# A Mamba state read out in the scan's own layout: half scans in place in PSUM, products with broadcast rows of C, accumulating transposes

## The reference

```
def step(h, ins):
    dt_t, u_t, B_t, C_t = ins
    h = jnp.exp(dt_t[..., None] * A) * h + (dt_t * u_t)[..., None] * B_t[:, None, :]
    y_t = jnp.einsum('bdn,bn->bd', h, C_t)
    return (h, y_t)
_, ys = jax.lax.scan(step, h0, xs)
y = jnp.moveaxis(ys, 0, 1) + u * Dp
y = y * jax.nn.silu(z)
```

## Time and profile before

| | |
|---|---|
| median of 3 runs | 2786.99 us (2777.39 to 2789.61) |
| the profiled execution's own time | 2776.09 us |
| its span | 2774.3 us |
| VectorE busy | 2444.0 us (88%) |
| TensorE busy | 2240.5 us (81%) |
| GpSimd busy | 1963.9 us (71%) |
| ScalarE busy | 1442.7 us (52%) |
| scan, 512 times | 1167.3 us |
| read_out, 1920 + 128 operations | 783.9 + 52.3 us |
| mean granted TensorE clock | 0.895 of full speed |
| DMA | 17.1% of 16 engines, 57 GB/s |

### The profile page before, as it was taken

How to read it: one execution, slowest core, us unless ns; L and a number is a source line. 1 busy time by engine, 2 the same in 40 slices (tenths; PEclk the granted TensorE clock), 3 DMA queues, 4 the chain that set the end, 5 groups by cost and what they waited for, 6 DMA issues and landing times. The chain is left out here.

```text
span 2774.3 us, 39442 instructions
## 1 busy us (share of the span) xinstructions
PE 2240.5 (81%) x10405; PEld 1427.0 (51%) x10405; DVE 2444.0 (88%) x4116; ACT 1442.7 (52%) x2468; POOL 1963.9 (71%) x1437
## 2 busy tenths in 40 slices
PE   3677888889788887978878797887978888897767
PEld 1344555555555454555545455554555555555544
DVE  1798998999899998999999899999989989999963
ACT  2545546555555555555565454655545555555423
POOL 1667868777776877768787686877777687777743
PEclk6778998989899898989989898998989989898989
DMA  2222121211212111121211112121121111112100
GB/s 77 68 69 65 54 70 50 66 54 54 69 46 69 52 54 63 54 69 46 69 54 54 61 53 69 53 69 46 54 69 53 61 54 58 57 54 71 46 25 4
DMA packets 83131, 158.16 MB, mean 57 GB/s; under 512 B 14420, under 2 KB 49076, under 8 KB 83012
## 3 DMA queue, kind: packets, MB, share of 16 engines
q1 hardware_dynamic: 83012, 157.01, 17.1%
HBM read 151.69 MB, written 5.29 MB: 57 GB/s over the span
## 5 line engine op out<-in xcount | busy, mean ns | idle before, releaser
L421 POOL TENSOR_TENSOR bt<-v,bb 128x1024 f32<-128x1024 f32 x512 | 1207.9, 2361 | 368.9 <-DVE h L773 366.1
L773 DVE TENSOR_TENSOR_SCAN h<-psA,bt 128x1024 f32<-128x1024 f32 x512 | 1167.3, 2280 | 70.6 <-issue 34.2
L598 ACT ACTIVATE psA<-dt,aneg 128x511 f32<-128x511 f32 x1024 | 665.0, 681 | 1037.7 <-DVE h L773 1034.6
L984 PE MATMUL psH<-ident,h 128*128 128x128 f32 x4096 | 657.2, 303 | 238.3 <-DVE acc L794 215.5
L794 DVE SCALAR_TENSOR_TENSOR acc<-psH,cc,acc 128x256 f32<-128x256 f32 x1920 | 783.9, 468 | 7.3 <-PE psH L984 7.1
L984 PEld LDWEIGHTS psH<-ident,h 128*128 128x128 f32 x4096 | 512.3, 154 | 530.2 <-DVE acc L794 354.9
L521 POOL TENSOR_TENSOR act<-pf,gf 128x512 f32<-128x512 f32 x288 | 365.9, 1270 | 149.0 <-DVE pf L878 128.6
L1067 PE MATMUL F<-h2T,w 128*128 128x512 f32 x576 | 347.5, 688 | 101.6 <-DVE pf L878 99.4
L1111 PEld LDWEIGHTS F<-w,act 128*128 128x128 f32 x2304 | 312.2, 201 | 110.2 <-issue 102.7
L1111 PE MATMUL F<-w,act 128*128 128x128 f32 x2304 | 322.4, 286 | 5.9 <-DVE facc L892 5.9
L1070 PE MATMUL F<-h2T,w 128*128 128x512 f32 x576 | 307.1, 616 | 0.0
(11 more groups left out here) (140 smaller groups left out, 1892.0 us busy)
## 6 DMA issues: line engine op xcount, KB each, us to landing
bb<-b_rows SPq DMA_DIRECT2D x256, 512.0 KB, 3.6
x<-in_L_attn_x SPq DMA_DIRECT2D x16, 256.0 KB, 3.3
xR<-in_L_attn_x SPq DMA_DIRECT2D x16, 256.0 KB, 2.9
out_x<-osb SPq DMA_DIRECT2D x16, 256.0 KB, 3.7
w<-in_L_ffn_ew SPq DMA_DIRECT2D x2, 1024.0 KB
modA<-mod_table SPq DMA_DIRECT2D x16, 128.0 KB, 3.6
modF<-mod_table SPq DMA_DIRECT2D x32, 64.0 KB, 2.6
b_rows<-xd SPq DMA_DIRECT2D x32, 32.0 KB, 1.6
```

The lines of the kernel that those rows point to most:

```text
L421: g.tensor_tensor(bt[:, n % 2, :, :], v[d][:, :, :], bb[:, n // 2 % 2, n % 2, :].unsqueeze(1).broadcast_to([P, NH, T]), ALU.mult).then_inc ...
L598: s.activation(decay[:, half, lo:hi], dt_[d][:, half, lo:hi], ACT.Exp, scale=aneg[d][:, half, n:n + 1]).then_inc(a_s, 1)
L773: w.tensor_tensor_scan(h[:, n % 2, :, :].rearrange("p k t -> p (k t)")[:, order], psA[:, order], bt[:, n % 2, :, :].rearrange("p k t -> p ...
L984: last = m.transpose(psH[:, i * E + half * P:i * E + half * P + P], h[:, n % 2, half, i * P:i * P + P], ident[:, :])
```

## The change

The read-out stays in the layout of the scan. In a slot, for each half: a scan of 512 elements *in place* in psA (so psA holds the state and not the decay), then g = psA * (row of C, broadcast over the partitions by a second DMA, `cb`) into SBUF. TensorE turns g by transposes that accumulate over the 16 states in `psY` (which takes the place of psH). After 16 states ScalarE copies psY into acc (`keep_y`), and `yg` now lies in acc's memory. `exps` of a half of step s+1 waits for the product g of that half of step s. C comes with B from one product (40 rows in place of 24), so CP and its copy go, and Z moves one slot earlier. The zero column goes.

```diff
-U_AT, XD_AT, DT_AT, LN1P_AT, CP_AT, Z_AT, V_AT = 0, 6, 7, 9, 9, 10, 11
+U_AT, XD_AT, DT_AT, LN1P_AT, Z_AT, V_AT = 0, 6, 7, 9, 9, 11
...
                 sp.dma_start(bb[:, pair % 2, :, :].rearrange("p n t -> p (n t)"), src.broadcast_to([P, 2 * T]))\
                     .then_inc(bb_in[pair % 2], 16)
+                wait(sp, g_s, 2 * used)
+                src = bc_dram[d, N + 2 * pair:N + 2 * pair + 2, :].rearrange("n t -> (n t)").unsqueeze(0)
+                sp.dma_start(cb[:, pair % 2, :, :].rearrange("p n t -> p (n t)"), src.broadcast_to([P, 2 * T]))\
+                    .then_inc(cb_in[pair % 2], 16)
...
             def bmul(step, d, n):
-                wait(pool, h_s, step - 1)
+                wait(pool, h_s, NH * (step - 1))
...
             def exps(step, b, d, n):
-                wait(act_e, h_s, step)
-                lo, hi, first = (1, T, 0) if d == 0 else (0, T - 1, T - 1)
-                decay = psA[:, :].rearrange("p (k t) -> p k t", t=T)
                 if n == 0:
                     act_e.wait_ge(dt_s, 2 * b + d + 1)
-                    s.activation(decay[:, :, first:first + 1], zero[:, :, :], ACT.Copy).then_inc(a_s, 1)
                 for half in range(NH):
-                    s.activation(decay[:, half, lo:hi], dt_[d][:, half, lo:hi], ACT.Exp,
+                    wait(act_e, g_s, NH * (step - 1) + half + 1)
+                    s.activation(psA[:, half * T:half * T + T], dt_[d][:, half, :], ACT.Exp,
                                  scale=aneg[d][:, half, n:n + 1]).then_inc(a_s, 1)
+
+            def keep_y(b, d):
+                act_e.wait_ge(y_s, STEPS * b + N * (d + 1))
+                wait(act_e, F2_full, (DOWN + NE) * (b - 1) + PROJ + 1)
+                for half in range(NH):
+                    s.activation(yg[d][:, half, :], psY[:, half * T:half * T + T], ACT.Copy).then_inc(acc_s, 1)
...
-                if k == CP_AT:
-                    take(b, piece(d, CP))
-                    s.activation(cc[d][:, :, :], psP[:, 0:NT * N], ACT.Copy).then_inc(pP_free, 1)
...
+                    if slot == 0 and ffn:
+                        keep_y(b - 1, 1)
+                    if slot == N and scan:
+                        keep_y(b, 0)
...
-            def scan(step, d, n, unit):
-                dve.wait_ge(a_s, NH * (step + 1) + unit)
+            def scan(step, d, n):
+                order = slice(None) if d == 0 else slice(None, None, -1)
                 dve.wait_ge(bt_s, step + 1)
-                wait(dve, pH_full, 2 * step - 2)
-                order = slice(None) if d == 0 else slice(None, None, -1)
-                w.tensor_tensor_scan(h[:, n % 2, :, :].rearrange("p k t -> p (k t)")[:, order], psA[:, order],
-                                     bt[:, n % 2, :, :].rearrange("p k t -> p (k t)")[:, order],
-                                     0.0, ALU.mult, ALU.add).then_inc(h_s, 1)
+                for half in range(NH):
+                    dve.wait_ge(a_s, NH * step + half + 1)
+                    ah = psA[:, half * T:half * T + T][:, order]
+                    w.tensor_tensor_scan(ah, ah, bt[:, n % 2, half, :][:, order], 0.0, ALU.mult, ALU.add)\
+                        .then_inc(h_s, 1)
+
+            def read_out(step, b, d, n):
+                wait(dve, y_s, step - 1)
+                if n % 2 == 0:
+                    dve.wait_ge(cb_in[n // 2 % 2], 128 * b + 64 * d + 16 * (n // 4) + 16)
+                for half in range(NH):
+                    dve.wait_ge(h_s, NH * step + half + 1)
+                    w.tensor_tensor(g_[:, n % 2, half, :], psA[:, half * T:half * T + T], cb[:, n // 2 % 2, n % 2, :],
+                                    ALU.mult).then_inc(g_s, 1)
...
-            def tr_h(step, n):
+            def sum_y(step, kept, n):
+                if n == 0:
+                    wait(pe, acc_s, kept)
+                for half in range(NH):
+                    pe.wait_ge(g_s, NH * step + half + 1)
+                    for i in range(NT):
+                        last = m.matmul(psY[:, half * T + i * P:half * T + i * P + P],
+                                        g_[:, n % 2, half, i * P:i * P + P], ident[:, :], is_transpose=True,
+                                        start=(n == 0 and i == 0), stop=(n == N - 1),
+                                        skip_group_check=True)
+                last.then_inc(y_s, 1)
...
```

More of the change, by code:

```diff
@@ L19 @@
 KINDS = 6
-U, XD, DT, CP, Z = 0, 2, 3, 5, 6
-PREP = 8
+U, XD, DT, Z = 0, 2, 3, 5
+PREP = 7
 PIECES = 1 + 2 * PREP + NH
@@ L132, in adaln_mamba_moe @@
         zs = [sb(f"zs{d}", [P, NH, T]) for d in range(2)]
-        xd = sb("xd", [R + N, T])
-        cc = [sb(f"cc{d}", [P, NT, N]) for d in range(2)]
+        xd = sb("xd", [R + 2 * N, T])
         xb = sb("xb", [P, NH, T])
@@ L141, in adaln_mamba_moe @@
         bt = sb("bt", [P, 2, NH, T])
-        zero = sb("zero", [P, NH, 1])
-        h = sb("h", [P, 2, NH, T])
-        acc = [sb(f"acc{d}", [P, NT, E]) for d in range(2)]
+        cb = sb("cb", [P, 2, 2, T])
+        g_ = sb("g", [P, 2, NH, T])
+        acc = [sb(f"acc{d}", [P, NH, NT, P]) for d in range(2)]
         def part(buf, rows, lo, shape):
@@ L234, in adaln_mamba_moe @@
         bb_in = [sem(f"bb_in{k}") for k in range(2)]
+        cb_in = [sem(f"cb_in{k}") for k in range(2)]
         bt_s = sem("bt_s")
@@ L237, in adaln_mamba_moe @@
         h_s = sem("h_s")
-        pH_full = sem("pH_full")
+        g_s = sem("g_s")
+        y_s = sem("y_s")
         acc_s = sem("acc_s")
@@ L264, in adaln_mamba_moe @@
         MOD_STEPS = 12
-        CONSTS = 10
+        CONSTS = 9
         block = ctx.enter_context(nc.Block())
@@ L930, in body @@
                     if scan_:
-                        scan(step, slot // N, slot % N, 2 * b + 1 + slot // N)
-                    if slot > 0 and scan_:
-                        read_out(step - 1, (slot - 1) // N, (slot - 1) % N, b)
-                    elif slot == 0 and ffn:
-                        read_out(step - 1, 1, N - 1, b - 1)
+                        scan(step, slot // N, slot % N)
+                        read_out(step, b, slot // N, slot % N)
                     if scan_:
@@ L976, in _ @@
             pe.wait_ge(halved, 7)
-            def tr_h(step, n):
-                pe.wait_ge(h_s, step + 1)
-                for i in range(NT):
-                    if i % 2 == 0:
-                        wait(pe, acc_s, NT * step - NT + i + 2)
-                    for half in range(NH):
-                        last = m.transpose(psH[:, i * E + half * P:i * E + half * P + P],
-                                           h[:, n % 2, half, i * P:i * P + P], ident[:, :])
-                    if i % 2 == 1:
-                        last.then_inc(pH_full, 1)
+            def sum_y(step, kept, n):
[9 more added lines that the diff above has]
+                last.then_inc(y_s, 1)
             def prep(b, d, k):
@@ L1006, in prep @@
                     for half in range(NH):
-                        last = m.matmul(psP[0:R + N, :], wxT[d][:, half, 0:R + N], u[d][:, half, :],
+                        last = m.matmul(psP[0:R + 2 * N, :], wxT[d][:, half, :], u[d][:, half, :],
                                         start=(half == 0), stop=(half == NH - 1))
-                    last.then_inc(pP_full, 1)
-                if k == CP_AT:
-                    open_piece(CP)
-                    for i in range(NT):
-                        for half in range(NH):
-                            last = m.matmul(psP[:, i * N:(i + 1) * N], u[d][:, half, i * P:i * P + P],
-                                            wxT[d][:, half, R + N:R + 2 * N], start=(half == 0), stop=(half == NH - 1))
                     last.then_inc(pP_full, 1)
@@ L1028, in skip_and_turn @@
                 for i in range(NT):
-                    last = m.matmul(bank[:, i * P:i * P + P], acc[d][:, i, half * P:half * P + P], ident[:, :],
+                    last = m.matmul(bank[:, i * P:i * P + P], acc[d][:, half, i, :], ident[:, :],
                                     start=False, stop=(i == NT - 1))
@@ L1121, in body @@
                     step = STEPS * b + slot
-                    if (slot > 0 and scan_) or (slot == 0 and ffn):
-                        tr_h(step - 1, (slot - 1) % N)
+                    if slot > 0 and scan_:
+                        sum_y(step - 1, 4 * b + 2 * ((slot - 1) // N), (slot - 1) % N)
+                    elif slot == 0 and ffn:
+                        sum_y(step - 1, 4 * b - 2, N - 1)
                     if ffn:
```

59 lines of the change are left out of this document (21 added, 38 removed).

## The result

| | before | changed |
|---|---|---|
| median | 2785.81 us (2777.39 to 2789.61, 4 runs) | 2804.83 us (2802.63 to 2809.09, 4 runs) |
| profiled execution, its span | 2776.09, 2774.3 | 2805.65, 2803.9 |
| VectorE busy | 2444.0 | 2302.2 |
| TensorE busy, mean granted clock | 2240.5, 0.895 | 2152.3, 0.916 |
| DMA | 17.1%, 57 GB/s | 31.0%, 105 GB/s |

The ratio is 1.0077, 95% interval 1.0054 to 1.0100: slower, as forecast, but by 0.8% and not by 2.2%.

The account below looks back on a forecast made before the run. VectorE was taken as the bound, with ScalarE's chain just beneath it in up slots. +4.34 per pass over 15 passes (+65), less 4 in pass 0, gave +61: 2837, forecast 2848; own range 2825 to 2880, stated range 2785 to 2925.

Parts of the forecast that it names:

- slot 31: Last slot of a pass: 3.47, then 3.49 from last facc over the loop's branch to next scan: 6.96.
- rival B: Half scans cost exactly their elements, 1.07 each: -4.2 per pass, 2785, no change; chance 8%.
- The chain: In up slots, from g over exponentials and tf to pf: at least 5.44 us pf to pf, before at least 4.77.
- rivals A: Half scans cost more than half: +58, 2906, or 2935 if the products pay more as well; chance 14%.
- Rival D: VectorE stays the bound in up slots, which shrink to 4.07 plus side work: 2672; chance 8%.
- Rival C: TensorE's new idle time in up slots costs it its clock, facc waits: +50 to +100, about 2920; chance 6%.
- Slot 29: ScalarE's 5.10 with logarithm and two table loads, about 0.35 more for the tanh of Z: 5.45.
- Slots 0 to 6: Start of a pass: 30.67 us where it was 31.54 before, -0.87 per pass.
- Slot 10: 4.07, the gate 2.24 and now a silu of Z, 0.60: 6.91, before 6.60.
- the 0.4% that I added: The median of before lies 0.4% above its profiled execution, so 2837 was raised to a forecast of 2848.
- the second broadcast DMA: 512 KB per two slots, issued at least 7.4 + 2.27 us before use, against 3.6 to landing: hidden.
- keep_y: Two ScalarE copies of 0.6 at slots 0 and 16, ahead of exponentials that wait for g anyway: hidden.

Follow-up runs that it names:

- experiment 9: The kernel before with its loop over the 13 middle batches written out: 2727.01 us, ratio 0.9786.
- experiment 10: The changed kernel with its loop over the 13 middle batches written out: 2785.02 us, ratio 0.9990 against the kernel before.
- Experiment 3: The changed kernel with Z put back one slot later, as in the kernel before: 2809.80 us, ratio 1.0081.
- Experiment 1: The changed kernel with the experts' tanh and copy (tf, gf) ahead of the exponentials on ScalarE in up slots 10 to 27: 2683.25 us, ratio 0.9625.
- experiment 8: The kernel before with one more ScalarE wait: exponentials for step s+1 start only after the first two readings of step s-1; 2984.21 us, ratio 1.0687.
- experiment 122: Not a run number: the 122 us by which Experiment 1, the changed kernel with tf and gf ahead of the exponentials, is below 2805; measured 2683.25 us.
- Experiment 7: The kernel of Experiment 1 with, besides, the first tanh of Z ahead of the logarithm on ScalarE: 2672.69 us, ratio 0.9592.

## Why the prediction was wrong in size

**The step that failed: slot 31.** It read "from the last facc over the loop's branch to the next scan 3.49 as before". Those 3.49 were taken for a constant and were not. The measured -2.90 of this slot splits so. VectorE's own work falls from 5.38 (the shortest slot 31 of experiment 9) to 4.47 (that of experiment 10): -0.91, which is about the forecast's -1.00. TensorE's lateness, 5.02 - 4.35 = 0.67, is gone. The pause was 2.64 and is 1.32: -1.32. The last two, 2.0 per pass, were not in the sum. Experiment 3 ties them to Z's move: with Z back in its place slot 31 is 8.34. The forecast did move Z, but only its work on VectorE; it did not ask where TensorE would wait instead.

Counted the other way, slot 31 missed its forecast by 1.90 per pass: 1.17 because the changed slot took 5.79 and not 6.96, and 0.73 because the one pass read for the slot before was a short one (7.96 against 8.69). Experiments 9 and 10 show the jump's part in the whole: write the loop out, and the change costs 57.5 us span against span, where +61 was forecast. That those two agree so closely is in part luck: there too slot 31 falls by 1.87 per pass where 1.00 was forecast, since TensorE is still late before, and slot 29 grows by 1.44 where 0.37 was forecast.

2804.83 lies inside the stated range by luck. Its lower end of 2785 was set for cheaper half scans (rival B), and the half scans cost what was forecast; that slot 31 could shrink by more than VectorE's own work was in no term and no rival.

**The chain: right.** Up slots 5.41 against 5.44 forecast, with facc or without; VectorE busy 2302 (below 2330); the wait of pf for tf 251 (about 260); half scans 1.12 start to start (1.13), products 0.60. So rivals A and B are out. The Trainium skill, "VectorE: DVE Perf Modes", section on the TRN2 errata, gives 120 cycles plus one for each element for an operation with a PSUM source, by its 0.96 GHz an estimate of 0.66 for 512 wide. The trace agrees for the duration of one product g (0.68) but not for what it costs in a row of them: two follow each other within 1.19, 0.60 each. The sum needed the second, as the prediction took it. Experiments 1 and 8 show the chain from both sides.

**Rival D: its mechanism was real, but not in this kernel.** It put the time at 2672 if tf were ready in time. Experiment 1 made tf ready and came out at 2683. That the two numbers are close is luck: rival D took 176 us off its base of 2848, the experiment 122 off 2805. Most of the 54 between them is GpSimd's bt, for which the scans of slots 14 to 16 then wait (0.43 to 1.26 each, 2.8 per pass, 42 us in 15 passes).

**Rival C: no.** The clock was granted at 0.95 in slots 11 to 16 and 1.00 in 19 to 27 of the changed kernel, as before. So the new idle time of TensorE in up slots did not lower its clock.

**Slot 29: under-sized.** 5.45 was ScalarE's queue; measured 6.53. The tanh of Z is not only one more item in that queue: VectorE waits for it behind the logarithm, and everything behind it on VectorE waits too. Experiment 7 took that out and got 5.50. This is +1.1 per pass against the forecast, the opposite sign to slot 31.

**Smaller terms.** Slots 0 to 6 gained 1.46, not 0.87: slot 1 alone 0.55, where 0.16 was given (4.86 in the pass read, 4.70 forecast); it is the second slot behind the jump and is uneven before (4.34 to 5.47). Slot 10 stayed at 6.6 instead of 6.9. The sum of all is 4.34 - 2.10 = 2.24 per pass; over 15 passes 34 us, which accounts for the 31 between +61 and the +29.6 measured span to span. The other 11 or so are the 0.4% that I added because the median of before lay above its profiled run; the changed kernel's does not.

**Hidden as said:** the second broadcast DMA. Nothing waits for cb; both rows land in about the same time as bb did, though the DMA share went up to 31%.

```profile
bb<-bc_rows SPq DMA_DIRECT2D x256, 512.0 KB, 4.2
cb<-bc_rows SPq DMA_DIRECT2D x256, 512.0 KB, 3.6
```

keep_y cost nothing either: slot 0, which has one, takes 3.69, and slot 3 without one 3.68.

## What to carry to other kernels

Work taken off the busiest engine is worth nothing while another engine's chain starts later because of it: find the instruction that the next engine is released by, and add up from there. When a change moves that release, look at the order behind it first; here a tanh ahead of two exponentials turned +0.8% into -3.8%, all against the kernel before as it stands. And an idle stretch at a loop's branch is not a constant of the loop: it depends on what waits ahead of it, so give it both ends, and take a mean over passes as the baseline, never one pass.
